# A graph layer on one core: 92 rows of main edges in 46 iterations, 54 early chunks in place of 71, and a new order at both ends of the loop

## The chip, the cores and the metric

The kernel runs on one core of a Trainium2 chip. The metric is the device time of one execution in microseconds (us), the median of several runs of the same program. The core has a matrix engine (TensorE, "PE" in the profile, with its weight loads as "PEld"), a vector engine (DVE), a scalar engine (ACT), GpSimd (POOL) and SyncE (SP). Each engine works through its own queue in the order of the program, and they meet only at semaphores.

## What is computed

A graph with N = 6250 nodes, 128 features and E = 106,250 edges, sorted by their destination `dst`; the last N edges of the unsorted list are loops from a node to itself. Every edge has one of three types.

```python
src_x = node_feature[edge_src]
parts = [relu(node_feature)]
for t in range(3):
    msg = relu(src_x @ W_e[t].T + b_e[t])
    msg = where(edge_type == t, msg, 0)
    parts.append(segment_sum(msg, edge_dst, num_segments=N))
agg = concatenate(parts, axis=1)
for t in range(3):
    updated = where(node_type == t, agg @ W_n[t].T + b_n[t], updated)
x = layernorm(x + updated + node_feature)
```

## The kernel before

**The table.** A message depends on the source node and the type alone, so PE, ACT and SP first build `message_table` in DRAM, N * 3 rows of 128 numbers (`make_batch`, `relu_half`, `store_half`, `store_last`). An edge is then a gather of one row.

**Main edges.** The first MAIN = HR * R = 90 * 1080 edges lie as 90 rows on 90 partitions. DVE removes the loops and 128 "dense" edges of each row (64 from each of two sets of 640 source nodes), closes the rows up to 896 slots (`close_up`, `unpack`, L1102 to L1105) and prepares indices and keys. PE turns them (`setup_unit`, L1556) and ACT copies them to `idx_t` and `key_t` (L798). The loop has NI = 45 iterations of two rows. An iteration has 14 columns, in four groups of 3, 4, 3 and 4: POOL gathers each column of 128 rows with one indirect DMA (L753), DVE makes the one-hots of a group (`one_hot`, L1252), PE sums the group with them (`sum_group`, L1652), and DVE adds the sums to `acc` (`add_sums`, L1264). The message buffer and the one-hots exist once, so POOL waits before it gathers group g of iteration j for the sum of group g of iteration j - 1:

```python
if j > 0:
    pool.wait_ge(group_summed, NG * (j - 1) + g + 1)
```

**Early edges.** The other 9,050 edges are ET = 71 chunks of 128. POOL gathers their rows of `x` into `xg` (L749) while the table is built, the calls from the 27th on held back by `msg_made`. PE turns, multiplies and sums them in NE = 36 pairs, one in each of the first iterations (`early_turn` L1614, `early_make` L1626 to L1631, `early_sum` L1640).

**Dense edges.** DVE picks two lists of 64 for each row (`list_dense`, L1131 and L1133, eight rounds each, run one after the other), unpacks them (`unpack_dense`, L1137 to L1146, whose L1142 signals `dense_keyed`), and later compares them with node numbers (`dense_onehot`, L1328). PE turns the keys (`dense_keys`, L1658), and for each iteration runs `dense_turn` (L1673), `dense_make` (L1686, L1690) and `dense_sum` (L1698). The turns come once in four quarters, and from iteration LEAD_FROM on once in three, so that the last is done in time.

**Tiles.** The 6250 nodes are 49 tiles of 128. Four are "extra": their edges are all early ones, and they use buffer set 1. A tile goes through ACT `finish_x` (L896), ACT `mask_selfs` (L912, the loops' messages), PE `finish_turn` (L1736) and `place_selfs` (L1713), DVE `finish_acc` (L1399), PE `finish_linear` (L1747, L1748 and the six of L1755), DVE `finish_h` (L1367 to L1375), ACT `finish_sd` (L917), DVE `finish_y` (L1381, L1383) and an SP store (L552, L568). `tile_step` puts tile t at iteration t + 3. Five tiles, 40 to 44, are still open in the last iteration, written out by hand as `last_iteration` on each engine.

**Order at the start of the loop.** On PE, `quarter(0, 0)` is `sum_group(0, 0)`, then `dense_keys()`, and only then `sum_group(0, 1)`. `dense_turn(0)` stands at the end of quarter (0, 3), ahead of `sum_group(1, 0)`. The change leaves these lines as they are:

```python
sum_group(j, g)
if q == 0:
    dense_keys()
```

Of the kernel before, what the change touches and what calls it, by code (L numbers as in the profile page):

```python
# [34 lines left out]
P = 128  # L35
# [5 lines left out]
R, HR, HC = 1080, 90, 7  # L41
# [3 lines left out]
KE = 4  # L45
# [54 lines left out]
SIDES = 2  # L100
# [17 lines left out]
QUADS = (NA - 1) // QUAD  # L118
BATCHES = ([(0, 1)] + [(1 + QUAD * m, QUAD) for m in range(QUADS)] + [(1 + QUAD * QUADS, NA - 1 - QUAD * QUADS)])
TAKEN_LATE, LATE = 3, 4  # L120
SPLIT = NA - TAKEN_LATE
Z0_TILES = SPLIT + 1
STORES = len(BATCHES) - 1 + TAKEN_LATE
SETS_OF_TILES = 4
assert sum(n for _, n in BATCHES) == NA and BATCHES[-1] == (SPLIT, TAKEN_LATE)
# [19 lines left out]
LEAD_FROM, LEAD_STEP = NE, 3  # L145
# [27 lines left out]

LIMIT_STEP = 15
# [12 lines left out]
LINEAR_AT = [next(q for q in range(at + 2, at + 6) if q % NG == 2) for at in EXTRA_AT]  # L187
# [6 lines left out]
assert PAIR_OF[-1] == NE - 1 and SLOT_OF[KE] + 1 + T <= ET  # L194


def tile_step(q, later):
    t = (q - later) // NG - (LATE - 1)
    return t if (q - later) % NG == 0 and 0 <= t < SPLIT else None
# [32 lines left out]
def build(nc, x, src, dst, etype, ntype, w_e, b_e, w_n, b_n, out):  # L232
# [6 lines left out]
    with ExitStack() as ctx:  # L239
# [59 lines left out]
        xg = sb("xg", [P, ET, D])  # L299
# [94 lines left out]
        iota_moved = sem("iota_moved")  # L394
        hot_iota_set, acc_zeroed, limits_set = sem("hot_iota_set"), sem("acc_zeroed"), sem("limits_set")
# [101 lines left out]
        def _(sp):  # L497
# [168 lines left out]
            for tile, tiles in BATCHES:  # L666
                if NI <= tile + tiles + LATE and tile + tiles <= SPLIT:
                    sp.wait_ge(fin_y[0], tile + tiles)
                    store_fin(tile, tiles)
            sp.wait_ge(fin_y[2], 1)  # L670
            store_fin(SPLIT)
            sp.wait_ge(fin_y[0], Z0_TILES)
            store_fin(SPLIT + 1)
            sp.wait_ge(ctl_set, 1)
            need = sp.value_load(ctl[0:1, 0:1], min_val=0, max_val=1)
# [37 lines left out]
        def _(pool):  # L713
# [13 lines left out]
                      allow_small_or_imprecise_dtypes=True)  # L727
# [54 lines left out]
        def _(act):  # L782
# [136 lines left out]
            def quarter(j, g):  # L919
# [13 lines left out]
                if g == 2 and j > 1:  # L933
                    mask_selfs(j - 2)
# [5 lines left out]
            def last_iteration():  # L940
                finish_x(0, 2, first=True)
                mask_selfs(SPLIT + 1)
                mask_selfs(SPLIT + 2)
                mask_selfs(ORDER[KE])
                finish_x(Z0_TILES - 1)
# [4 lines left out]
                finish_sd(Z0_TILES - 1)  # L950
# [22 lines left out]
        def _(dve):  # L973
# [151 lines left out]
            def list_dense(s):  # L1125

                for k in range(DENSE // 8):
# [754 lines left out]
```

## Time and profile before

| what | us |
|---|---|
| median of 3 runs (905.99 to 906.22) | 906.05 |
| the profiled execution | 907.5 |
| its span, first to last instruction | 905.7 |
| PE busy in it | 716.2 (79%) |
| POOL busy in it | 673.7 (74%) |
| DVE busy in it | 616.4 (68%) |
| mean granted TensorE clock | 0.912 |

Busy time leaves out the time in which an engine's sequencer prepares or waits. A row of the timeline has the start, the length, the engine, the line, the operation, what it writes and reads, its shape and how many instructions were merged; in brackets stand the engine's idle time before it and what ended it ("issue": nothing that the profile shows).

### The profile page before, as it was taken

How to read it: one execution, taken by the hardware profiler on the slowest of the kernel's cores; microseconds unless marked ns; L12 is line 12 of the kernel's file. 1: busy time of each engine (PE TensorE's matmuls, PEld its weight loads, DVE VectorE, ACT ScalarE, POOL GpSimd, SP SyncE). 2: the span in 40 equal slices, each digit the busy share in tenths (PEclk: the TensorE clock that was granted, in tenths of full speed). 3: DMA queues.
4: the chain of work that ended last, by engine and by line, in shares of the span. 5: the costliest groups of instructions: out<-in, count | busy, mean ns of one | idle time of the engine just before them, and what ended most of it. 6: DMA issues, size and time to landing. Idle time of an engine off the chain costs nothing.

```text
span 905.7 us, 14050 instructions
## 1 busy us (share of the span) xinstructions
PE 716.2 (79%) x4555; PEld 598.9 (66%) x4555; DVE 616.4 (68%) x1468; ACT 145.0 (16%) x397; POOL 673.7 (74%) x719
## 2 busy tenths in 40 slices
PE   5593056887997988888898878989888798769786
PEld 3362056776876876676687766878767587658674
DVE  7999988476676557557575754775675477656656
ACT  3393000111111101111110120110112011001120
POOL 7777777777777777777777777777777777777772
PEclk9796569998999989999999998999899999989989
DMA  8595533433443343343344342434435334324321
GB/s 245 161 311 147 136 97 76 113 97 50 146 117 105 97 110 107 103 111 92 94 118 116 96 115 78 121 107 111 106 96 114 93 85 118 102 63 128 97 53 45
DMA packets 72065, 101.39 MB, mean 112 GB/s; under 512 B 18137, under 2 KB 55517, under 8 KB 71995
## 3 DMA queue, kind: packets, MB, share of 16 engines
q0 software_dynamic: 22432, 45.99, 21.3%
q1 hardware_dynamic: 46861, 50.45, 18.5%
q10 hardware_dynamic: 2702, 4.08, 1.5%
q8 instruction: 37, 0.61, 0.3%
q14 instruction: 33, 0.27, 0.1%
HBM read 87.47 MB, written 12.97 MB: 111 GB/s over the span
## 4 chain that ended last, share of the span: by engine, by line
POOL 44%; PE 18%; issue 16%; DVE 15%; DMA 6%; SPq 0%; DVEq 0%; POOLq 0%; ACT 0%; ACTq 0%
POOL tab L753 44%; DMA tab<-message_table,idx_t 5%; PE ps L1652 5%; PE ps L1755 3%; PE ps L1673 3%; DVE src_wide L1098 1%; DVE stage L1131 1%; PE ps L1690 1%; PE ps L1686 1%; DVE first_wide L1034 1%; PE ps L1748 1%; DMA dst_raw<-in_dst 1%; PE ps L1631 1%; DVE dst_raw L1091 1%; PE ps L1698 1%
## 5 line engine op out<-in xcount | busy, mean ns | idle before, releaser
L753 POOL DMA_INDIRECT tab<-message_table,idx_t x630 | 595.2, 945 | 194.1 <-issue 185.6
L1652 PE MATMUL ps<-work,tab 128*128 128x126 f32 x1260 | 180.4, 286 | 94.0 <-DMA tab<-message_table,idx_t 68.7
L1252 DVE TENSOR_TENSOR work<-key_t,ps 128x378 f32<-128x378 f32 (+1 forms) x180 | 108.8, 606 | 208.3 <-PE ps L1652 203.7
L1652 PEld LDWEIGHTS ps<-work,tab 128*128 128x128 f32 x1260 | 163.6, 199 | 106.2 <-issue 68.4
L1264 DVE TENSOR_TENSOR acc<-ps,acc 128x126 f32 (+1 forms) x306 | 96.2, 314 | 30.0 <-DVE acc L1264 9.9
L1755 PE MATMUL ps<-wn_t,stage 128*128 128x384 f32 x282 | 104.8, 512 | 0.0
L749 POOL DMA_INDIRECT xg<-in_x,esrc_t x67 | 72.4, 1081 | 20.7 <-issue 16.8
L1755 PEld LDWEIGHTS ps<-wn_t,stage 128*128 128x128 f32 x282 | 56.3, 200 | 40.4 <-issue 5.6
L1673 PE MATMUL ps<-first_wide,tab 128*128 128x128 f32 x450 | 62.8, 291 | 9.5 <-DVE first_wide L1328 6.5
L1673 PEld LDWEIGHTS ps<-first_wide,tab 128*128 128x128 f32 x450 | 58.9, 207 | 9.9 <-issue 9.9
L896 ACT ACTIVATE stage<-ps 128x128 f32<-128x128 f32 x47 | 12.9, 277 | 297.0 <-PE ps L1755 282.1
L1673 PE MATMUL ps<-dense_f,tab 128*128 128x128 f32 x450 | 60.0, 283 | 0.0
L1673 PEld LDWEIGHTS ps<-dense_f,tab 128*128 128x128 f32 x450 | 56.6, 200 | 0.0
L1370 DVE SCALAR_TENSOR_TENSOR h<-ps,mask,h 128x128 f32<-128x128 f32 x147 | 51.6, 351 | 6.7 <-PE ps L1755 1.5
L1626 PE MATMUL ps<-we_t,emsg 128*128 128x128 f32 x216 | 36.3, 312 | 23.0 <-issue 20.4
L917 ACT ACTIVATE sd<-mv,eps 128x1 f32<-128x1 f32 x49 | 14.3, 294 | 230.2 <-DVE mv L1375 230.2
L1626 PEld LDWEIGHTS ps<-we_t,emsg 128*128 128x128 f32 x216 | 32.0, 220 | 27.0 <-issue 23.8
L1686 PE MATMUL ps<-we_t,order_f 128*128 128x128 f32 x270 | 44.1, 308 | 6.5 <-DVE acc L1264 6.5
L1573 PE MATMUL ps<-we_t,work 128*128 128x384 f32 x98 | 44.5, 540 | 3.3 <-DVEq L995 3.2
L1686 PEld LDWEIGHTS ps<-we_t,order_f 128*128 128x128 f32 x270 | 40.7, 225 | 8.1 <-issue 7.8
L1690 PE MATMUL ps<-we_t,order_f 128*128 128x128 f32 x270 | 44.2, 302 | 0.0
L1338 DVE TENSOR_TENSOR order_f<-ps,dst_raw 128x768 f32<-128x768 f32 x45 | 42.7, 949 | 0.1
(260 smaller groups left out, 1021.4 us busy)
## 6 DMA issues: line engine op xcount, KB each, us to landing
tab<-message_table,idx_t POOLq DMA_INDIRECT x630, 2.6
message_table<-tab SPq DMA_DIRECT2D x24, 384.0 KB, 3.5
dst_raw<-dense_types SPq DMA_DIRECT2D x45, 192.0 KB
wn_raw<-message_table SPq DMA_DIRECT2D x22, 384.0 KB, 3.4
src_wide<-dense_lists SPq DMA_DIRECT2D x45, 128.0 KB, 3.2
we_raw<-early_types SPq DMA_DIRECT2D x18, 192.0 KB
be_b<-early_types SPq DMA_DIRECT2D x18, 192.0 KB
work<-in_x ACTq DMA_DIRECT2D x10, 256.0 KB, 5.0
```

Of the source, the lines that this page charges most:

```text
L749: pool.indirect_dma_start(xg[:, q, :], None, x, bass.IndirectOffsetOnAxis(ap=rows, axis=0)).then_inc(x_gathered, 16)
L753: pool.indirect_dma_start(msg[:, slot, :], None, table, bass.IndirectOffsetOnAxis(ap=rows, axis=0)).then_inc(signal, 16)
L1252: dve.tensor_tensor(hot[:, first:first + n, :].rearrange("p c (t w) -> p c t w", w=WIN), keys.broadcast_to((P, n, T, WIN)), iota_win.rearr ...
L1264: dve.tensor_tensor(cols, sums.rearrange("p (t c) -> p t c", t=T), cols, ALU.add).then_inc(added, 1)
L1370: fin_link(dve.scalar_tensor_tensor(h[z][:, :], lin_bank(z, nth)[:, t * D:(t + 1) * D], mask[:, t, at(tile)], h[z][:, :], ALU.mult, ALU.ad ...
L1573: pe.matmul(ps[:, MSG_PS + i, 0:T * D], xt[:, par, i, :], we_t[:, :], start=True, stop=False)
L1626: pe.matmul(early_made[:, 0, :], exm[:, 0, t, :], we_t[:, t * D:(t + 1) * D], start=(t == 0), stop=False)
L1652: ins = pe.matmul(sums_bank(j, g), msg[:, column, :], hot[:, column, :], start=(c == 0), stop=(c == n - 1))
L1673: ins = pe.matmul(dxt_ps[:, :, s * DENSE:(s + 1) * DENSE], dx[:, (SETS - 1 - s) * DT + k, :], donehot[s][:, k, :, :], start=(k == 0), stop ...
L1686: pe.matmul(dmsg_ps[:, 0, :], dxm[:, 0, t, :], we_t[:, t * D:(t + 1) * D], start=(t == 0), stop=False)
L1690: ins = pe.matmul(dmsg_ps[:, 1, :], dxm[:, 1, t, :], we_t[:, t * D:(t + 1) * D], start=False, stop=(t == T - 1))
L1755: ins = pe.matmul(lin, stage[z][:, i, :], wn_t[:, i, :], start=False, stop=(i == T))
```

## The change

HR goes from 90 to 92 and KE, the number of extra tiles, from 4 to 3. From this follow NI = 46, MAIN = 99,360, ET = 54, NE = 27, and 644 table gathers and 54 early gathers where there were 630 and 71. PE waits for `masks_set` after the turning of indices and keys, no more before it. DVE does four rounds of the first dense list, then the one-hots of iteration 0, then the other twelve rounds. Tiles are laid out by `tile_turns`: as before up to tile 33, and from tile 34 on up to one iteration sooner. LEAD_FROM is NI - 9 = 37 (36 before). In the last iteration four tiles are open, 42 to 45, none but tile 45 waits for the last group's sum, and the order of all engines is new.

```diff
-R, HR, HC = 1080, 90, 7
+R, HR, HC = 1080, 92, 7
-KE = 4
+KE = 3
-QUADS = (NA - 1) // QUAD
+QUADS = (NA - 3) // QUAD
-TAKEN_LATE, LATE = 3, 4
+TAKEN_LATE, LATE = 2, 4
-LEAD_FROM, LEAD_STEP = NE, 3
+LEAD_FROM, LEAD_STEP = NI - NG * 2 - 1, 3
+def tile_turns():
+    at = []
+    for t in range(SPLIT):
+        if t < LEAD_FROM - LATE + 1:
+            at.append(NG * (t + LATE - 1))
+        else:
+            at.append(max(NG * (t + LATE - 2), turn_at(t + 1) + ADD_LATER - ACC_LATER, at[-1] + NG - 1))
+    return at
+def tile_step(q, later):
+    return TILES.get(q - later)
@@ sync, the last stores
-            sp.wait_ge(fin_y[2], 1)
-            store_fin(SPLIT)
-            sp.wait_ge(fin_y[0], Z0_TILES)
-            store_fin(SPLIT + 1)
+            sp.wait_ge(fin_y[0], Z0_TILES)
+            store_fin(SPLIT - 1)
             sp.wait_ge(ctl_set, 1)
             need = sp.value_load(ctl[0:1, 0:1], min_val=0, max_val=1)
-            store_extra(KE)
+            sp.wait_ge(fin_y[2], 1)
+            store_fin(SPLIT)
             sp.wait_ge(fin_y[3], 1)
             store_fin(NA - 1)
+            store_extra(KE)
@@ vector, finish_h
+                if isinstance(nth, int) and nth > 0:
+                    dve.wait_ge(fin_y[z], nth)
@@ vector, last_iteration
                 dve.wait_ge(group_summed, NG * j + 2)
-                finish_h(SPLIT - 1, SPLIT - 1)
-                dve.wait_ge(group_summed, NG * j + 3)
                 add_sums(j, 0, bases_of[0])
                 add_sums(j, 1, bases_of[1])
-                finish_acc(SPLIT + 1, Z0_TILES - 1, 0, ADDED["main", j, 1])
+                finish_acc(NA - 1, 0, 3, ADDED["main", j, 1])
+                finish_h(SPLIT - 1, SPLIT - 1)
                 finish_h(SPLIT, 0, 2)
+                finish_y(SPLIT - 1, SPLIT - 1)
+                dve.wait_ge(group_summed, NG * j + 3)
                 add_sums(j, 2, bases_of[2])
-                finish_y(SPLIT - 1, SPLIT - 1)
                 finish_y(SPLIT, 0, 2)
+                finish_h(NA - 1, 0, 3)
                 dve.wait_ge(group_summed, NG * j + 4)
                 add_sums(j, 3, bases_of[3])
                 finish_acc(ORDER[KE], KE, 1, ALL_ADDS)
-                finish_acc(NA - 1, 0, 3, ALL_ADDS)
-                finish_h(SPLIT + 1, Z0_TILES - 1)
+                finish_y(NA - 1, 0, 3)
                 finish_h(ORDER[KE], KE, 1, slot=SLOT_OF[KE])
-                finish_y(SPLIT + 1, Z0_TILES - 1)
-                finish_h(NA - 1, 0, 3)
                 finish_y(ORDER[KE], KE, 1, slot=SLOT_OF[KE])
-                finish_y(NA - 1, 0, 3)
@@ vector, ahead of the loop
-            list_dense(0)
-            list_dense(1)
+            list_dense(0, range(DENSE // 16))
             dve.wait_ge(iota_moved, 1)
             dve.wait_ge(setup_copied, len(UNITS))
             for g in range(NG):
                 one_hot(0, g)
+            list_dense(0, range(DENSE // 16, DENSE // 8))
+            list_dense(1, range(DENSE // 8))
             unpack_dense()
@@ tensor, last_iteration, from the second group on
                 sum_group(j, 1)
-                finish_linear(0, 2, first=True)
-                pe.wait_ge(stage_acc[2], 1)
-                finish_turn(SPLIT + 1, Z0_TILES - 1, len(BATCHES))
                 pe.wait_ge(added, ADDED["dense", j, SIDES - 1])
                 finish_turn(NA - 1, 0, len(BATCHES), 3, first=True)
                 pe.wait_ge(fin_var[1], KE)
                 finish_turn(ORDER[KE], KE, NZ, 1)
+                place_selfs(NA - 1, 0, 3)
+                place_selfs(ORDER[KE], KE, 1)
+                finish_linear(0, 2, first=True)
                 pe.wait_ge(added, ADDED["main", j - 1, NG - 1])
                 sum_group(j, 2)
-                place_selfs(SPLIT + 1, Z0_TILES - 1)
-                place_selfs(NA - 1, 0, 3)
-                place_selfs(ORDER[KE], KE, 1)
+                finish_linear(0, 3, first=True)
                 pe.wait_ge(hot_ready, NG * NI)
                 pe.wait_ge(d_hot, NI)
+                linear_open(KE, 1)
                 pe.wait_ge(added, ADDED["main", j, 1])
-                linear_open(KE, 1)
                 sum_group(j, 3)
-                finish_linear(Z0_TILES - 1)
                 linear_types(KE, 1)
-                finish_linear(0, 3, first=True)
@@ tensor, ahead of the loop
-            pe.wait_ge(masks_set, 1)
             pe.wait_ge(tab_ready, 2 * NB + 1)
             pe.wait_ge(rows_set, 1)
             setup_unit(IDX_UNIT, KEY_UNIT)
             pe.wait_ge(keys_set, 1)
             setup_unit(KEY_UNIT, len(UNITS))
+            pe.wait_ge(masks_set, 1)
```

Besides this, `xg` is kept large enough for the extra tiles' slots, the batches of tile loads are cut as (2, then 4 each, then 3), and POOL makes the limit that row 91 is held against with one more small instruction. In the main loop `finish_linear` stands ahead of `place_selfs`.

## Rows read from the trace of the kernel before

**Rows 1.** The page: busy time of each engine, and the group of the table gathers.
```profile
PE 716.2 (79%) x4555; PEld 598.9 (66%) x4555; DVE 616.4 (68%) x1468; ACT 145.0 (16%) x397; POOL 673.7 (74%) x719
...
L753 POOL DMA_INDIRECT tab<-message_table,idx_t x630 | 595.2, 945 | 194.1 <-issue 185.6
```

**Rows 2.** Timeline of POOL: the 54th early gather, the first table gather.
```profile
78.46 1.18 POOL L749 DMA_INDIRECT xg<-in_x,esrc_t  x1 [0.30 <-issue]
...
101.54 0.94 POOL L753 DMA_INDIRECT tab<-message_table,idx_t  x1 [0.30 <-issue]
```

**Rows 3.** Waits of POOL: total us, times, longest.
```profile
POOL tab L753 <- PE ps L1652: 8.4, 21, 1.1
```

**Rows 4.** Timeline of POOL: table gathers 18, 29, 564 and the last, 630.
```profile
122.79 0.94 POOL L753 DMA_INDIRECT tab<-message_table,idx_t  x1 [0.30 <-issue]
...
136.53 0.94 POOL L753 DMA_INDIRECT tab<-message_table,idx_t  x1 [0.30 <-PE ps L1652]
...
805.58 0.94 POOL L753 DMA_INDIRECT tab<-message_table,idx_t  x1 [0.85 <-PE ps L1652]
...
889.53 0.94 POOL L753 DMA_INDIRECT tab<-message_table,idx_t  x1 [0.30 <-issue]
```

**Rows 5.** Timeline of PE, from the turned indices to the second iteration.
```profile
88.50 1.28 PE L1556 MATMUL ps<-ident,first_wide 90*128 90x90 f32 x7 [14.38 <-DVE mask L1245]
...
114.74 1.65 PE L1652 MATMUL ps<-work,tab 128*128 128x126 f32 x6 [23.19 <-DVE work L1252]
...
117.55 0.41 PE L1658 MATMUL ps<-ident,stage 90*128 90x90 f32 x1 [1.16 <-DVE stage L1142]
...
117.75 4.20 PE L1652 MATMUL ps<-work,tab 128*128 128x126 f32 x22
...
128.70 2.48 PE L1673 MATMUL ps<-first_wide,tab 128*128 128x128 f32 x10 [6.52 <-DVE first_wide L1328]
...
133.10 3.14 PE L1652 MATMUL ps<-work,tab 128*128 128x126 f32 x20
```

**Rows 6.** Timeline of ACT: indices copied to `idx_t`.
```profile
89.22 1.42 ACT L798 ACTIVATE idx_t<-ps 128x270 int32<-128x270 f32 x2 [13.43 <-PE ps L1556]
```

**Rows 7.** Timeline of DVE over the same stretch.
```profile
82.97 0.62 DVE L1104 TENSOR_SCALAR first_wide<-loop_f 90x896 f32<-90x896 int32 x1
...
117.20 0.29 DVE L1142 SCALAR_TENSOR_TENSOR stage<-stage 90x128 f32<-90x128 int32 x1
...
120.37 0.55 DVE L1252 TENSOR_TENSOR work<-key_t,ps 128x378 f32<-128x378 f32 x1 [1.10 <-PE ps L1652]
...
128.47 0.82 DVE L1328 TENSOR_TENSOR dense_f<-src_wide,ps 128x640 f32<-128x640 f32 x1
```

**Rows 8.** Sums of one stretch: engines' busy us, granted clock, DMA share, GB/s.
```profile
100.00:120.00 20.00, 4.10 (x18) 3.81 (x19) 18.32 (x45) 1.81 (x1) 15.13 (x16) 0.50 0.28 73
```

**Rows 9.** Timeline of PE: the last extra tile's linear in the leading stretch.
```profile
795.84 0.32 PE L1747 MATMUL ps<-bn_parts,pick_parts 128*128 128x384 bf16 x1 [3.17 <-DVE mv L1375]
...
796.65 3.79 PE L1755 MATMUL ps<-wn_t,stage 128*128 128x384 f32 x6
```

**Rows 10.** Timeline of the end: PE, DVE, the last store.
```profile
884.33 0.33 PE L1747 MATMUL ps<-bn_parts,pick_parts 128*128 128x384 bf16 x1
...
885.13 2.10 PE L1755 MATMUL ps<-wn_t,emsg 128*128 128x384 f32 x6
...
892.19 0.49 PE L1652 MATMUL ps<-work,tab 128*128 128x126 f32 x2 [0.31 <-DMA tab<-message_table,idx_t]
...
893.14 0.56 DVE L1399 TENSOR_TENSOR stage<-acc,ps 128x384 f32<-128x384 f32 x1
...
900.21 1.12 DVE L1370 SCALAR_TENSOR_TENSOR h<-ps,mask,h 128x128 f32<-128x128 f32 x3 [0.36 <-PE ps L1755]
...
902.69 0.35 DVE L1383 TENSOR_SCALAR xg<-h,mv,rstd 128x128 f32<-128x128 f32 x1
...
903.52 0.36 SPq L552 DMA_DIRECT2D out<-xg  x1
```

More of the change, by code:

```diff
@@ L186 @@
 EXTRA_AT = [extra_at(n) for n in range(KE)]
-LINEAR_AT = [next(q for q in range(at + 2, at + 6) if q % NG == 2) for at in EXTRA_AT]
+LINEAR_AT = [next(q for q in range(at + 2, at + 8)
+                  if (q % NG == 2 or q >= NG * LEAD_FROM) and tile_step(q, LINEAR_LATER) is None
+                  and tile_step(q - 1, LINEAR_LATER) is None) for at in EXTRA_AT]
 EXTRAS = {at: n for n, at in enumerate(EXTRA_AT)}
@@ L193 @@
 assert all(LIMIT_FIRST + LIMIT_STEP * (PAIR_OF[n] + 1) >= (NA + 2 + n) * P for n in range(KE - 1))
[L194 to L199, printed above, removed]
+assert PAIR_OF[-1] == NE - 1 and SLOT_OF[KE] + 1 + T <= NT + 2 * (1 + T)
 def count_adds():
@@ L932, in quarter @@
                     dense_relu(dense_step(q, MAKE_LATER))
-                if g == 2 and j > 1:
-                    mask_selfs(j - 2)
+                if tile_step(q, -2) is not None:
+                    mask_selfs(tile_step(q, -2))
+                if q == NG * (NI - 1) - 2:
+                    mask_selfs(SPLIT)
                 if q + 2 in EXTRAS:
@@ L1123, in spans, with list_dense @@
                 dve.tensor_tensor(tail, tail, penalty[:, :], ALU.add).then_inc(keys_set, 1)
-            def list_dense(s):
-                for k in range(DENSE // 8):
+            def list_dense(s, rounds):
+                for k in rounds:
                     first, last = dense_window(k)
@@ L1437, in quarter @@
                     self_masks()
-                if tile_step(q, ACC_LATER) is not None:
-                    finish_acc(tile_step(q, ACC_LATER), tile_step(q, ACC_LATER), 0, ADDED["main", j - 1, NG - 1])
+                t = tile_step(q, ACC_LATER)
+                if t is not None:
+                    finish_acc(t, t, 0, max(ADDED["main", t + 1, NG - 1], ADDED["dense", t + 1, SIDES - 1]))
                 if q - 1 in EXTRAS:
@@ L1764, in batches_up_to @@
             def batches_up_to(tile):
-                return sum(first <= max(tile, 1) for first, _ in BATCHES)
+                return sum(first <= max(tile, BATCHES[1][0]) for first, _ in BATCHES)
             def quarter(j, g):
@@ L1785, in quarter @@
                     finish_linear(t, first=t == 0, behind=extras if extras else None)
+                t = tile_step(q, 1)
+                if t is not None:
+                    place_selfs(t, t)
                 if q in EXTRA_LINEAR:
                     n = EXTRA_LINEAR[q]
-                    done = sum(tile_step(before, LINEAR_LATER) is not None for before in range(q))
+                    done = sum(tile_step(before, LINEAR_LATER) is not None for before in range(q + 1))
                     finish_linear(n, 1, first=n == 0, behind=done)
```

31 lines of the change are left out of this document (16 added, 15 removed).

## The prediction

> **What bounds the kernel now.** I read the page first, and there PE looks like the busiest engine, 79% against POOL's 74% [rows 1]. That is misleading: each table gather counts 0.945 us as busy, and in front of nearly every one stand 0.30 us more that wait for nothing, 185.6 of the 194.1 us of idle time in that group [rows 1]. So I read POOL's timeline next. A gather costs 1.25 us from start to start, the first table gather starts at 101.54 [rows 2] and the last at 889.53 [rows 4]. These are 629 steps in 787.99 us, 1.253 each: POOL practically never stops from the beginning of the kernel to 16 us before its end. The view of waits says how much it waits for others: 21 times for PE's sums, 8.4 us in total [rows 3]. Each such entry holds the usual 0.30, so the real part is 8.4 - 6.3 = 2.1 us; the one at gather 564 shows 0.85 where 0.30 is usual [rows 4]. Take the 2.1 out of the stretch from gather 29 to gather 630 (136.53 to 889.53, 601 steps [rows 4]) and a free step is 750.9 / 601 = 1.2494 us. PE and DVE can be late only by making POOL wait, and after POOL's last gather.
>
> So the change is judged by three numbers: when POOL gets going, how many gathers it then has to issue, and what is left behind the last.
>
> **The counts.** 71 early gathers become 54 and 630 table gathers 644: three fewer in all, 3.7 us. This gain exists only if POOL starts its table gathers 17 steps sooner and is not stopped afterwards.
>
> **When the first table gather can start.** POOL ends the 54th early gather at 79.6 [rows 2]; I leave the pace up to there as it is. The table isn't what it waits for: its last part is sent before that, and in the trace of before nothing was waited for at 101.54. The indices are. DVE writes them until 82.97 + 0.62 = 83.6 [rows 7], but PE turns them only at 88.50, 14.38 us idle, released by the masks [rows 5]. With the wait for the masks moved behind, PE starts at 83.8, ACT's two copies end (89.22 + 1.42) - 88.50 = 2.14 later [rows 5, 6], at 85.9, and POOL starts at about 86.2, 15.3 us sooner. The same two turns and copies run as before, only 4.7 us sooner. What else is pulled ahead of the masks, the keys, must still wait for DVE's key work and is hidden under the lists.
>
> **What stops it: the 18th gather.** POOL then has free columns for iteration 0 (14) and, once group 0 of iteration 0 is summed, for 3 more. The new place of the one-hots buys just that: they are there half a list after 88, around 98, well ahead of gather 15 at 86.2 + 14 * 1.25 = 103.7. Gather 18 would start at 107.4. It belongs to group 1 and waits for the sum of group 1 of iteration 0. On PE `dense_keys` stands in front of that sum, and it waits for `dense_keyed`, which DVE signals after all sixteen rounds of both lists. In the trace this is seen directly: PE does the six records of group 0 at 114.74, then is released by DVE's L1142 for the transpose at 117.55, and only at 117.75 goes on [rows 5]; L1142 starts at 117.20 [rows 7]. Neither the lists' rounds nor the four one-hots get fewer or shorter: windows of the lists go by R = 1080, and DVE works 18.32 of the 20 us from 100 to 120 [rows 8]. So `dense_keyed` stays at 117.5. The sum of group 1 is 8 of the 22 records of 4.20 us from 117.75 on, 1.5 us, or 2.2 at the pace of 114.74 (six in 1.65) [rows 5]. With the usual 0.30, gather 18 starts at 119.6 to 120.3; I take 120.0. Before, it started at 122.79 [rows 4]. POOL stands for some 12.6 us, and of 15.3 us only 2.8 are left. This also answers what the moved waits cost: up to 12 us of delay of the indices would not be seen.
>
> **The 29th gather.** It is the first of iteration 2 and waits for the sum (1, 0). That sum is on PE behind `dense_turn(0)`, which starts at 128.70 after 6.52 us of idleness, released by DVE's one-hot of L1328 [rows 5, 7], and the sum starts at 133.10 [rows 5]. DVE is the pacer here: its chain of key work, lists, row bases (the 1.10 us before 120.37 [rows 7]; the sum named there had ended at 116.4) and loop lists doesn't change. The sum's six records take 0.94 us as their share of 20 in 3.14, or 1.65 as at 114.74 [rows 5]: done at 134.0 to 134.75, gather 29 at 134.3 to 135.1, taken as 134.8. By POOL's own pace it would be 120.0 + 11 * 1.25 = 133.7, so the wait decides. Before it was 136.53 [rows 4]. What is left of the earlier start is 1.7 us, and it can be between 1.4 and 2.2.
>
> PE runs this stretch at the lower of its two clock levels: granted 0.50 in 100:120 [rows 8], 1.2 GHz. The Trainium skill ("TensorE: Matmul & The Clock Gate", section "Part 1: The HAM clock gate") has the throttled clock as the default, which activity releases; by that rule the sum pulled ahead to 98 doesn't help, since PE is idle again until 117.5. The trace agrees, with 0.50 after 23.19 us of idleness; at full clock `dense_turn(0)` would be over some 2 us sooner and so would gather 29, and the sum would be 2 us less.
>
> **The loop.** From gather 29 there are now 644 - 29 = 615 steps: 615 * 1.2494 = 768.4, so the last gather starts at 134.8 + 768.4 = 903.2. The early work ends 9 iterations sooner, but it was PE's and DVE's and hidden under POOL: nothing.
>
> **The 2.1 us of stalls** came around gather 564, where the fourth extra tile's linear stood in the stretch of three-quarter turns: PE waited 3.17 us for DVE at 795.84 and its next six matmuls took 3.79 us at the fallen clock, 2.10 elsewhere [rows 9, 10]. That tile is gone, and so is this cause (it is already out of the 1.2494). New in its place is one more main tile in the nine last iterations. A tile's linear is 2.9 us of PE (884.33 to 887.23 [rows 10]), spread over some 150 us; I see no single place where it piles up. New stalls lie between 0 and the 2.1 of before; I take 0.5. Last gather: 903.7. The new `fin_y` wait in `finish_h` is for DVE's own earlier instruction, two quarters back: nothing.
>
> **The end.** Before, the kernel ended 905.7 - 889.53 = 16.2 us after the last gather started [rows 4, 10]: landing and sum at +2.7 (892.19), then on PE two whole linears and a half one. Now tile 44 needs no sum of the last two groups, and behind the last sum stands only half a linear. But PE has the other linears ahead of it. From the end of group 1's sum, at -5.2 (884.33), it does eight transposes (1.4 by estimate, 1.0 to 2.0), a linear (2.75), group 2 (0.8, half of the 1.65 at half clock), a linear (2.75), the opening of tile 45 (885.13 - 884.33 = 0.8), group 3 (1.0): it is through at +4.3 instead of +3.15. From there: DVE's last add and `finish_acc` (892.68 to 893.70: 1.0), six matmuls (1.95), DVE and ACT from L1370 to the tile's end (900.21 to 903.04: 2.85, and 0.1 before), the store (905.7 - 903.52 = 2.2) [rows 10]. Sum: 12.4. If PE weren't the bound, 11.3; if it waits on ACT or DVE as well, up to 14.5.
>
> **Sum.** 903.7 + 12.4 = 916.1 for the span of 905.7: +10.4. Against the profiled execution's own 907.5 that is 917.9; the 1.8 around the span stays. That execution lay 1.45 above the median of the runs, so the median becomes 906.05 + 10.4 = 916.4. In short: fourteen gathers more, +17.5; start, -1.7; old stalls, -2.1, new ones, +0.5; end, -3.8.
>
> **Rivals.**
> 1. *POOL runs through (faster).* If nothing stopped it from 86.2 on, the last gather would start at 86.2 + 643 * 1.2494 = 889.6, the end come at 902.0, the median at 902.3. The point from which this decides is `dense_keyed` at 107.4 or sooner, together with the dense turn ten us sooner. For it speaks that indices, table and group 0 are ready; against it 117.20 and 117.55 in [rows 5, 7], and that I find no instruction taken out of that chain.
> 2. *The leading stretch stalls more.* With early work gone after iteration 26, PE has less to do in ten iterations, its clock may fall in more of them, and then the closer tiles meet a slow PE, as at 796.65, where six matmuls lost 1.7 us and the waits came to 2.1 [rows 3, 9]. Two or three such events cost 2 to 5 us: 918.5 to 921. The same page of the Trainium skill speaks for it: idleness brings the clock down. Against it: POOL's lead over PE is refilled in each iteration, and three extra tiles earlier in the loop cost nothing.
> 3. *The end isn't shortened*, because PE's pile of linears in front of the last sum takes as long as what was taken from behind it: +3.8, 920.2.
> 4. *Nothing measurable*: needs a chain on DVE ten us shorter without POOL being free throughout, for which nothing speaks.
>
> **Chances.** The forecast 0.76, with a range of its own from 914.5 to 918.5 (start 1.4 to 2.2, new stalls 0 to 2.1, end 11.3 to 14.5). Rival 1: 0.05. Rival 2: 0.10. Rival 3: 0.07. Rival 4: 0.02. A change of 0.2% (1.8 us) is about what a measurement of this kernel can tell from none. Slower is the forecast with rivals 2 and 3: 0.93; faster 0.05; same 0.02. The range is 913.5 to 920.5: it takes in the forecast, rival 3 and the lower half of rival 2.
>
> **What would show it.** In the new trace: POOL's first table gather near 86.2 with an idle time of some 6 us before it, released by ACT's copy; an idle time of about 12 us before the 18th, released by PE, with PE's transpose near 117.5 just ahead; a wait of 1 us before the 29th, at 134.8; the last gather near 903.5; the end some 12.4 us after. The prediction is wrong if gather 18 starts long before 119, if the loop's step isn't 1.25, or if POOL's waits after gather 29 come to more than 2 us.

## The result and the profile after

The changed kernel takes 940.77 us (median of 4 runs, 935.38 to 942.1), the one before, measured beside it, 906.13 (905.99 to 906.55): 1.037 times as long, 95% interval 1.0328 to 1.0412. Forecast were 916.4 and a range up to 920.5. The change is slower, as forecast, but by 34.6 us and not by 10.4. The ratios leave out slow runs, of which there was one below, 3772.36 us for the kernel with its loads cut into 75 and 15 rows.

The page of the profiled execution (its own time 941.7; line numbers of the changed kernel, the table gather is L773 now):

```profile
span 939.8 us, 13789 instructions
...
PE 724.6 (77%) x4451; PEld 606.0 (64%) x4451; DVE 609.4 (65%) x1455; ACT 142.7 (15%) x389; POOL 667.4 (71%) x717
...
L773 POOL DMA_INDIRECT tab<-message_table,idx_t x644 | 608.3, 945 | 233.8 <-issue 191.4
```

Against [rows 1], POOL's share fell from 74% to 71%. POOL, which paced the kernel before, has stood still somewhere. Its timeline shows where:

```profile
84.81 0.94 POOL L769 DMA_INDIRECT xg<-in_x,esrc_t  x1 [0.30 <-PE ps L1594]
...
101.51 1.07 POOL L773 DMA_INDIRECT tab<-message_table,idx_t  x1 [15.75 <-ACT idx_t L818]
...
135.09 0.94 POOL L773 DMA_INDIRECT tab<-message_table,idx_t  x1 [12.55 <-PE ps L1672]
...
149.49 0.94 POOL L773 DMA_INDIRECT tab<-message_table,idx_t  x1 [0.97 <-PE ps L1672]
...
810.51 0.94 POOL L773 DMA_INDIRECT tab<-message_table,idx_t  x1 [1.64 <-PE ps L1672]
...
826.55 0.94 POOL L773 DMA_INDIRECT tab<-message_table,idx_t  x1 [2.61 <-PE ps L1672]
...
831.95 0.94 POOL L773 DMA_INDIRECT tab<-message_table,idx_t  x1 [1.96 <-PE ps L1672]
...
844.18 0.94 POOL L773 DMA_INDIRECT tab<-message_table,idx_t  x1 [3.80 <-PE ps L1672]
...
926.91 0.94 POOL L773 DMA_INDIRECT tab<-message_table,idx_t  x1 [0.30 <-issue]
```

The shape at the start is the forecast one: a wait for ACT's copy of the indices before the first table gather, 12.55 us before the 18th, 0.97 before the 29th, each released by what was named. But each of them is late: 101.51 for the forecast 86.2, 135.09 for 120.0, 149.49 for 134.8. After the 29th come five waits for PE between 810 and 850: 1.64, 2.61, 1.96, 3.80 and, at 849.47, 0.60, each with the usual 0.30 in it, 9.1 us net.

The span grew by 34.1 us. Of this the 29th gather gives +13.0 (149.49 against 136.53 in [rows 4]), fourteen more steps of 1.2494 give +17.5, stalls after the 29th gather +6.9 (926.91 - 149.49 - 615 * 1.2494 = 9.0, where before had 2.1), the tail -3.3 (939.8 - 926.91 = 12.9 for 16.2). Against the forecast span of 916.1, 23.7 us are unaccounted for: 14.7 at the 29th gather, 8.5 in stalls, 0.5 in the tail.

**Why the start is late.** DVE's first instruction on the edges waits for four transfers that SP issues: the three loads of destinations, sources and types, and behind them one number for each row (0.4 KB), the destination that follows the row's last:

```profile
4.32 0.33 SPq L531 DMA_DIRECT2D dst_raw<-in_dst  x1
...
5.44 0.56 SPq L532 DMA_DIRECT2D dst_raw<-in_dst  x1
```

The chain of waits names the fourth, which goes by the same tile name (start, length, what), and DVE waits for it:

```profile
5.44 23.72 DMA dst_raw<-in_dst
```

```profile
29.18 1.27 DVE L1046 TENSOR_REDUCE low<-dst_raw 92x1 f32<-92x1080 int32 x1 [17.80 <-DMA dst_raw<-in_dst]
```

Before, the same piece of the chain, and the sizes of its transfers with the time from issue to landing, read:

```profile
5.62 7.38 DMA dst_raw<-in_dst
...
13.02 1.27 DVE low L1027
```

```profile
dst_raw<-in_dst SPq DMA_DIRECT2D x1, 379.7 KB, 4.7
...
typ_raw<-in_edge_type SPq DMA_DIRECT2D x1, 379.7 KB, 7.2
...
dst_raw<-in_dst SPq DMA_DIRECT2D x1, 0.4 KB, 7.4
```

DVE starts 16.2 us later. The 29th gather comes 120.3 us after DVE's start, and the forecast had put it at 134.8 - 13.0 = 121.8. It was the three loads that became slow. In the trace's own records of DMA packets each row of 1080 numbers is one packet of 4320 bytes. Before, the 270 rows of the three loads move from 6.77 to 11.87 us; in the changed kernel the 276 rows move from 6.59 to 28.02. The loads are 2% larger and take four times as long.

**Why POOL stalls late.** PE's waits from 740 to 880 (sum in us, times, longest):

```profile
PE ps L1756 <- DVE stage L1420: 15.8, 4, 5.6
```

L1756 is `finish_turn`, and L1420 the last instruction of DVE's `finish_acc` for the tile before. `finish_turn` writes the PSUM columns that this `finish_acc` still has to read, so PE waits for it. PE's own timeline, and DVE's over the same stretch:

```profile
811.13 1.72 PE L1672 MATMUL ps<-work,tab 128*128 128x126 f32 x14
...
818.45 0.45 PE L1756 MATMUL ps<-ident,xg 128*128 128x128 f32 x1 [5.59 <-DVE stage L1420]
...
836.17 0.45 PE L1756 MATMUL ps<-ident,xg 128*128 128x128 f32 x1 [3.82 <-DVE stage L1420]
```

```profile
810.27 0.68 DVE L1271 TENSOR_TENSOR work<-key_t,ps 128x504 f32<-128x504 f32 x1 [6.36 <-PE ps L1672]
...
816.11 0.55 DVE L1271 TENSOR_TENSOR work<-key_t,ps 128x378 f32<-128x378 f32 x1 [0.85 <-issue]
...
817.75 0.56 DVE L1420 TENSOR_TENSOR stage<-acc,ps 128x384 f32<-128x384 f32 x1 [0.28 <-DVE acc L1283]
```

PE ends two groups' sums at 812.85, then stands until DVE has worked through one quarter (from 810.27) and most of the next (from 816.11), where `finish_acc` of the tile before ends at 817.75 + 0.56. DVE began only at 810.27, having stood 6.36 us for a sum of PE's. So the two take turns in waiting, and the next sum, and with it POOL's next free columns, is behind `finish_turn` in PE's queue.

`finish_acc` of a tile stands two quarters behind its `finish_turn`. With tiles four quarters apart PE therefore has two quarters between that `finish_acc` and the next tile's turn, with three apart only one. The changed kernel has four such short steps, at tiles 34, 35, 37 and 38, and the wait occurs four times.

### The profile page after: what moved, and what is told of

It is laid out like the page before. It is cut to its first block, busy times and chain, and to the rows that moved or that the text cites. A ratio compares the mean times of both kernels' runs of the same rounds, so it can differ in the third digit from the quotient of the medians.

```text
span 939.8 us, 13789 instructions
## 1 busy us (share of the span) xinstructions
PE 724.6 (77%) x4451; PEld 606.0 (64%) x4451; DVE 609.4 (65%) x1455; ACT 142.7 (15%) x389; POOL 667.4 (71%) x717
## 4 chain that ended last, share of the span: by engine, by line
POOL 42%; PE 19%; DVE 17%; issue 16%; DMA 5%; DVEq 1%; SPq 0%; ACT 0%; ACTq 0%
POOL tab L773 42%; PE ps L1693 4%; PE ps L1672 4%; PE ps L1775 3%; DMA dst_raw<-in_dst 3%; DMA tab<-message_table,idx_t 2%; PE ps L1710 2%; PE ps L1706 1%; DVE src_wide L1117 1%; DVE stage L1150 1%; PE ps L1768 1%; DVE h L1391 1%; DVE acc L1283 1%; DVE first_wide L1053 1%; PE ps L1718 1%
## 5 line engine op out<-in xcount | busy, mean ns | idle before, releaser
L773 POOL DMA_INDIRECT tab<-message_table,idx_t x644 | 608.3, 945 | 233.8 <-issue 191.4
L1672 PE MATMUL ps<-work,tab 128*128 128x126 f32 x1288 | 190.2, 293 | 86.7 <-DMA tab<-message_table,idx_t 75.1
L1672 PEld LDWEIGHTS ps<-work,tab 128*128 128x128 f32 x1288 | 173.1, 204 | 101.4 <-issue 90.7
L1693 PE MATMUL ps<-first_wide,tab 128*128 128x128 f32 x460 | 69.2, 306 | 6.0 <-DVE first_wide L1347 5.5
L769 POOL DMA_INDIRECT xg<-in_x,esrc_t x50 | 53.2, 1064 | 24.5 <-PE ps L1594 13.2
L1693 PEld LDWEIGHTS ps<-first_wide,tab 128*128 128x128 f32 x460 | 65.5, 222 | 6.5 <-issue 6.5
L1693 PEld LDWEIGHTS ps<-dense_f,tab 128*128 128x128 f32 x460 | 59.4, 205 | 0.0
L1706 PE MATMUL ps<-we_t,order_f 128*128 128x128 f32 x276 | 47.1, 317 | 6.8 <-DVE acc L1283 6.8
L1710 PE MATMUL ps<-we_t,order_f 128*128 128x128 f32 x276 | 47.5, 313 | 0.0
L932 ACT ACTIVATE wn_raw<-wn_raw,smask 128x128 f32<-128x128 f32 x135 | 43.8, 390 | 0.0
L1718 PE MATMUL ps<-first_wide,dense_f 128*128 128x216 f32 x184 | 41.4, 347 | 1.6 <-DVE first_wide L1367 1.6
```

What stands on the lines that cost most here:

```text
L769: pool.indirect_dma_start(xg[:, q, :], None, x, bass.IndirectOffsetOnAxis(ap=rows, axis=0)).then_inc(x_gathered, 16)
L773: pool.indirect_dma_start(msg[:, slot, :], None, table, bass.IndirectOffsetOnAxis(ap=rows, axis=0)).then_inc(signal, 16)
L1672: ins = pe.matmul(sums_bank(j, g), msg[:, column, :], hot[:, column, :], start=(c == 0), stop=(c == n - 1))
L1693: ins = pe.matmul(dxt_ps[:, :, s * DENSE:(s + 1) * DENSE], dx[:, (SETS - 1 - s) * DT + k, :], donehot[s][:, k, :, :], start=(k == 0), stop ...
L1706: pe.matmul(dmsg_ps[:, 0, :], dxm[:, 0, t, :], we_t[:, t * D:(t + 1) * D], start=(t == 0), stop=False)
L1710: ins = pe.matmul(dmsg_ps[:, 1, :], dxm[:, 1, t, :], we_t[:, t * D:(t + 1) * D], start=False, stop=(t == T - 1))
```

## The experiments

Two theories were put against the slowdown. A: the loads of the edges are slow because of their number of rows, 92. B: the late stalls come from `finish_turn` standing right behind the sum in the stretch where tiles are three quarters of an iteration apart. Rival to A: any load of this size with more rows, or the other work pulled forward, does it. Rival to B: the lower clock, or DVE's amount of work.

The Trainium skill ("DMA: Bandwidth & Descriptors", section "Why a DMA increments its semaphore by 16 and not by 1") says that a transfer is spread over the largest number of engines, at most 16, that divides the slowest dimension of both its sides: 15 for 90 rows, 4 for 92, 16 and 12 for 80 and 12. That named theory A. No view names the engines of one transfer, but the packet records show how many rows of edges are in flight at once. In the changed kernel it is four at most for 21.3 of the 21.4 us; in the kernel before 15 is the commonest number (2.2 of 5.1 us). The trace agrees with the rule.

**The load in two parts**, in the changed kernel, rows 0 to 79 and 80 to 91. DVE now waits for seven transfers, not four; the last of them, the 92 single numbers, is left as it was:

```diff
-sp.dma_start(raw[:, :], dram[0:MAIN].rearrange("(p c) -> p c", c=R)).then_inc(got_edges, 16)
+for first, last in ((0, 80), (80, HR)):
+    sp.dma_start(raw[first:last, :], dram[first * R:last * R].rearrange("(p c) -> p c", c=R)).then_inc(got_edges, 16)
```

> The changed kernel with one edit: each of the three loads of edges is sent as two, rows 0 to 79 and rows 80 to 91, where it was one of 92 rows. Theory A (the number of rows of one load decides over how many DMA engines it is spread; 90 rows divide by 15, 92 by 4 at most, 80 by 16, 12 by 12): the loads land near 13 us again where they land at 29.2, DVE begins its chain near 13, POOL's 18th table gather starts near 120 (135.1 now) and the 29th near 135 (149.5 now), and the median falls by 15 us to about 926. Rival (the loads are late for another reason, such as the ACT queue's own loads at that time or the 2% more bytes): DVE still begins at 27 or later and the median stays near 940.

Measured: 927.9 (923.42 to 929.73), 1.0216 of before (1.0188 to 1.0243), 12.9 us under the changed kernel.

```profile
16.97 1.27 DVE L1048 TENSOR_REDUCE low<-dst_raw 92x1 f32<-92x1080 int32 x1 [4.89 <-DMA dst_raw<-in_dst]
...
PE ps L1758 <- DVE stage L1422: 17.6, 4, 5.6
```

DVE starts 12.2 us sooner, the 29th gather comes at 137.58, 11.9 sooner. The rows of the loads now end at 12.68, and 15 or 16 of them are in flight for 2.6 of 6.4 us. The late waits (here L1758 and L1422) are untouched. Theory A held, with 12.9 us where 15 was expected: the start lies 4 us later than the expected 13; 9.2 us of stalls stay.

**The same in the kernel before**, loads cut into 76 and 14 rows (by the rule 4 and 14 engines):

> The kernel before with one edit: its three loads of edges are sent as rows 0 to 75 and rows 76 to 89, where each was one load of 90 rows. 76 rows divide by 4 at most, 14 by 14. Theory A: most of the bytes go as slowly as in the changed kernel; DVE begins its chain 10 to 16 us later than at 13.0, everything up to POOL's 29th table gather moves by as much, and the median rises by 10 to 16 us, to 916 to 922. Rival (size or count of loads does not matter): 906, within 1 us.

Measured: 918.07, 1.0123 (1.0106 to 1.014), 11.2 us over before (906.85 in that batch), with 90 rows and nothing else changed. The rows of the loads end at 27.94, for 11.87 in the kernel before.

```profile
29.35 1.27 DVE L1029 TENSOR_REDUCE low<-dst_raw 90x1 f32<-90x1080 int32 x1 [17.23 <-DMA dst_raw<-in_dst]
```

**Cut into 75 and 15 rows** instead, as many transfers:

> The kernel before with its three loads of edges sent as rows 0 to 74 and rows 75 to 89. It has as many loads as the run that sent 76 and 14 rows, and both 75 and 15 divide by 15. Theory A: DVE starts on the edges at 13 to 17 us and the median is 905 to 908. Rival (the number of loads, not the divisor, cost the 11 us): 915 or more.

```profile
14.13 1.27 DVE L1029 TENSOR_REDUCE low<-dst_raw 90x1 f32<-90x1080 int32 x1 [2.02 <-DMA dst_raw<-in_dst]
```

Measured: 908.12 against 908.38, ratio 0.9993 (0.9983 to 1.0003). Neither the cutting nor a part of some 75 rows costs anything measurable; how the number of rows divides does.

**The kernel before once more**, for its spread:

> The kernel before, unchanged, profiled once more beside the three others of this group. DVE's first instruction on the edges starts at 13.0 us in the profile of before and at 16 to 17 in four of the five variants with whole or split fast loads. If that is the chip and the moment, this profile will have it at 15 to 17 as well, with a span within 1 us of 906; if it is something of the changed kernel, it will have it at 13.0 to 13.5.

Measured: 909.18 in one run, DVE's first instruction at 14.59 (13.02 in the profile shown). Over all kernels with 90 undivided rows this start lies between 13.0 and 16.1, with 92 rows cut 80 and 12 between 15.9 and 17.0. Most of that spread is the fourth transfer. With 90 rows in the changed kernel (the next run, DVE at 16.05) the types land as soon as before, 7.5 us after issue for 7.2, and the single numbers 3 us later:

```profile
typ_raw<-in_edge_type SPq DMA_DIRECT2D x1, 379.7 KB, 7.5
...
dst_raw<-in_dst SPq DMA_DIRECT2D x1, 0.4 KB, 10.4
```

With 92 rows cut 80 and 12 the rows of the loads end between 12.2 and 14.3 us and DVE starts 2.5 to 4.3 us behind them; with 90 rows uncut it is 1.2 to 2.0. Cutting the fourth transfer too was not tried.

**90 rows in the changed kernel** (HR 90, KE 4, all else as changed):

> The changed kernel with HR and KE set back to 90 and 4, and so 630 table gathers, 71 early ones and 45 iterations; the start's and the end's new order and the sooner tiles stay. Theory: the first table gather starts at 101.5 as before and the 29th at 136.5; the tail after the last gather is about 12.5 instead of 16.2; the sooner tiles bring POOL waits in the stretch of three-quarter turns, 5 to 10 us in place of 2.1. Sum: 906 - 3.7 + 3 to 8 = 905 to 910. Rival (POOL's waits there come from PE's thinner work after iteration 27 and not from the tiles' places): they stay near 2 us and the median is 902 to 903.

Measured: 927.32, 1.0222 (1.0205 to 1.0239). The expectation of 905 to 910 was missed. The start is mended (DVE at 16.05, 29th gather 137.03), but POOL stalls 26 us after it:

```profile
PE ps L1756 <- DVE stage L1420: 16.1, 4, 4.5
...
PE ps L1767 <- DVE mv L1396: 5.8, 1, 5.8
```

The short steps are four here too, and PE's waits at them as long as with 92 rows (16.1 us for 15.8), so the closer turns are costly without the 92 rows. New is the wait of 5.8 us: a fourth extra tile stands in this stretch, and its linear is one quarter ahead of a main tile's. POOL's longest stall, 7.6 us, lies right behind that wait.

**The turn at the end of PE's quarter** (with the load in two parts):

```diff
-                if t is not None:
+                if t is not None and q < NG * LEAD_FROM:
                     finish_turn(t, t, batches_up_to(t), first=t == 0)
...
+                t = tile_step(q, 0)
+                if t is not None and q >= NG * LEAD_FROM:
+                    finish_turn(t, t, batches_up_to(t))
```

> The kernel of the split load with one edit: in the stretch of three-quarter turns PE does a tile's finish_turn as the last thing of its quarter, behind linear, dense make and dense turn, where it stood right behind the group's sum. Theory B (POOL's waits in that stretch come from PE standing at finish_turn for DVE's finish_acc of the tile before, which with tiles three quarters apart belongs to the quarter just ended): PE's waits for DVE's finish_acc there, 17.6 us with the split load, fall under 5, POOL's waits after its 29th gather fall from 9.2 us to under 4, the median falls by 5 us or more. Rival (they come from the fallen clock and the thin work on PE whatever the order): POOL's waits stay at 7 to 11 us, the median within 2 us of the split load's.

Measured: 919.84 (919.21 to 921.85), 1.015 (1.0129 to 1.017), 8.1 us under the kernel with the loads cut alone.

```profile
PE ps L1758 <- DVE stage L1422: 1.5, 1, 1.5
```

17.6 us of waits became 1.5, and POOL's stalls after the 29th gather became nothing, with no matmul and no instruction of DVE's removed. Theory B held. The clock moved with it. The window from 800 to 860 in the kernel with only the loads cut, and in this one (window, length, busy time of PE, its loads, DVE, ACT and POOL, granted clock, DMA share, GB/s):

```profile
800.00:860.00 60.00, 48.02 (x293) 40.98 (x292) 36.49 (x87) 5.87 (x21) 39.38 (x43) 0.89 0.34 87
```

```profile
800.00:860.00 60.00, 53.02 (x339) 45.34 (x338) 38.79 (x91) 7.01 (x25) 45.36 (x49) 0.92 0.40 104
```

The clock rose from 0.89 to 0.92 once PE stood less, and in the kernel before it is 0.93 there. So the lower clock goes with the waits; what share of the 8.1 us came through it wasn't measured by itself.

The size of the stalls isn't fixed. Four kernels have the same order in this stretch, and their profiled executions have 9.1 us of stalls (the changed kernel), 9.2 (loads cut), 3.6 and 5.3 (the two edits at the start, below). The runs of each of them spread over 3.8 to 6.7 us, with the turn moved over 2.6. That the one makes the other is likely, but only one execution of each kernel has a profile.

**The tiles elsewhere**: the load in two parts, and the tiles brought forward one quarter each at tiles 28, 32, 38 and 41, four quarters apart otherwise. This line takes the place of the `if` and `else` in `tile_turns`:

```diff
+at.append(NG * (t + LATE - 1) - sum(t >= sooner for sooner in (28, 32, 38, 41)))
```

> The kernel of the split load with other tile turns: each of the tiles 28, 32, 38 and 41 comes a quarter sooner after its forerunner and all others four quarters apart, where the changed kernel has five steps of three quarters from tile 34 to 38. The last tiles have the places they have in the changed kernel. Theory B: most steps are four quarters again; POOL's waits after its 29th gather fall from 9.2 us to 1 to 5, the median falls by 4 to 8 us. Rival (fallen clock, thin work): they stay at 7 to 11 us.

Measured: 923.38, 1.0181 (1.0164 to 1.0198). The stalls fell from 9.2 to 1.4 (1.45 and 0.50, less the usual 0.30 each), but the tail grew from 12.8 to 15.0: 4.5 us better than the close turns, 3.5 worse than moving the instruction. The expectation counts five short steps in the changed kernel; by its `tile_turns` they are four, as many as here, but close together there. PE's waits for `finish_acc` from 540 to 900, and the window from 800 to 860:

```profile
PE ps L1755 <- DVE stage L1419: 15.8, 6, 4.6
...
800.00:860.00 60.00, 50.63 (x315) 43.08 (x314) 33.21 (x79) 7.19 (x24) 45.37 (x49) 0.89 0.39 100
```

PE still waits 15.8 us for `finish_acc`, six times, and POOL hardly notices. So such a wait alone isn't the price; it is paid where the waits follow each other closely. And the granted clock is 0.89, as low as with the loads alone cut, while POOL works 45.37 us of the 60 for 39.38: the lower clock by itself doesn't stop POOL there.

**The same with 90 rows** (27, 31, 37, 40, uncut loads). The edit also loosens the rule for the extra tiles' linears, which puts the third extra tile's at quarter 137, one ahead of a main tile's (138 in the other kernels with 90 rows):

```diff
-                  if (q % NG == 2 or q >= NG * LEAD_FROM) and tile_step(q, LINEAR_LATER) is None
+                  if (q % NG == 2 or q >= NG * 27) and tile_step(q, LINEAR_LATER) is None
```

> The changed kernel with 90 rows and 4 extra tiles, and the tile turns spread as in the run beside it (a quarter sooner at tiles 27, 31, 37 and 40). Nothing is left of the change but the start's order, spread sooner tiles and the new last iteration. Theory B: POOL's waits, 26 us in the run with 90 rows, fall to 1 to 6 us, the tail after the last gather is 12.5 to 13.5 us where it was 16.2 before; the median is 903 to 908. Rival (the extra tile at iteration 38 is what makes the 26 us): they stay above 12 us, the median above 914.

Measured: 937.18, 1.0334 (1.0317 to 1.0352); missed by far, and the rival's numbers came true. POOL stalls 34 us. PE's waits from 540 to 900:

```profile
PE ps L1764 <- DVE mv L1393: 17.5, 5, 5.4
...
PE ps L1753 <- DVE stage L1417: 15.2, 6, 3.3
```

L1764 begins a tile's linear and waits until DVE has the statistics of the tile whose sums share its PSUM bank. With four extra tiles among the moved ones this handover is too close as well. How much of the 34 us is the tile count and how much the third linear's new place wasn't separated, and PE also stood 13.0 us, four times, for nothing that the profile shows.

**90 rows, with the turn and the extra tile's linear last:**

> The changed kernel with 90 rows and 4 extra tiles, and in the stretch of three-quarter turns PE does finish_turn and the extra tile's linear as the last things of their quarter. Theory B: POOL's waits, 26 us with 90 rows alone, fall under 4 us, the tail after the last gather is 12.5 to 14; the median is 902 to 908, 20 us under the run with 90 rows alone. Against the kernel with 92 rows and finish_turn last (919.8) the fourteen gathers and the later start of the table gathers weigh 13 to 18 us. Rival: with a fourth extra tile there the waits stay above 10 us whatever the order, 915 or more.

Measured: 918.65, 1.011 (1.0095 to 1.0125), where 902 to 908 was expected. The turn's waits are gone (L1756 1.1 in all), the next one in line is not:

```profile
818.43 0.48 PE L1767 MATMUL ps<-bn_parts,pick_parts 128*128 128x384 bf16 x1 [5.78 <-DVE mv L1396]
```

One quarter behind the extra tile's linear comes a main tile's, and waits 5.78 us for DVE's statistics of the former. POOL stalls 16.3 us in all, 8.9 of them right behind this wait; the 7.4 ahead of it weren't traced to a cause. The rival had it right here: above 10 us and 915 or more, whatever the order.

**The start undone** (the loads cut, `masks_set` and the one-hots where they were before):

> The kernel of the split load with the two edits at the start undone: PE waits for the masks ahead of the turning of indices, and the one-hots of iteration 0 stand behind both lists. Theory of the prediction (the 18th and the 29th gather are held by the dense keys and the dense turn, whatever lies ahead of them): gathers 18 and 29 start within 0.5 us of where they do with the split load alone, and the medians agree within 1 us. Rival (the edits save what they were put in for): the 29th gather and the median are 2 us or more later than with the split load alone.

Measured: 929.35 (924.5 to 930.95), 1.0254 (1.0237 to 1.0271). The 29th gather comes 120.4 us after DVE's start, 120.6 with the edits, so they save nothing there; only the stop moves, to the 15th gather, which waits 8.55 us (with the usual 0.30). The medians lie 1.45 us apart (1 was expected), less than either kernel's own spread.

**`dense_keys` later on PE** (the loads cut, at quarter 2 instead of 0):

> The kernel of the split load with one edit: PE turns the dense keys two quarters later, after the sum of group 2 of iteration 0. Theory of the prediction (the dense keys hold the 18th gather, the dense turn and DVE's next one-hots hold the 29th): the 18th gather starts by 12 us or more sooner than the 123.3 of the split load, as soon as POOL reaches it, and the 29th no sooner than 0.5 us; the median is within 1.5 us of the split load's. Rival (the stop at the 18th gather is what costs): the 29th gather starts 2 us or more sooner too, and the median falls with it.

Measured: 926.32, 1.0225 (1.0203 to 1.0247).

```profile
109.94 0.94 POOL L775 DMA_INDIRECT tab<-message_table,idx_t  x1 [0.30 <-issue]
...
122.18 0.94 POOL L775 DMA_INDIRECT tab<-message_table,idx_t  x1 [3.80 <-PE ps L1674]
...
136.34 0.94 POOL L775 DMA_INDIRECT tab<-message_table,idx_t  x1 [9.47 <-PE ps L1674]
```

The 18th gather starts 13 us sooner and waits for nothing. The wait turns up 7 and 11 gathers later instead (3.50 and 9.17 us net), and the 29th is 120.5 us behind DVE's start as ever. The median is 1.6 us under that of the loads cut alone, where 1.5 was the limit expected; the runs of the two kernels overlap, and DVE started 1.1 us sooner in this profile. So removing a stop before the one that DVE sets gained nothing measurable.

**Where the old 2.1 us were.** The prediction laid them on the extra tile's linear. In the kernel before, that linear alone last in its quarter:

> The kernel before with one edit: the linear of the extra tile in the stretch of three-quarter turns stands last in its quarter on PE. Theory: PE's wait of 3.2 us for DVE there goes, POOL's three waits near its 564th to 578th gather, 2.0 us together, go with it, and the median falls by 1 to 2 us, to 904 to 905.5. Rival (the waits come from the fallen clock of that stretch, not from the place of the linear): the median stays within 0.5 us of before.

```profile
PE ps L1747 <- DVE mv L1375: 3.2, 1, 3.2
```

Measured: 908.06 against 908.38, 0.9999 (0.9988 to 1.0009); the 3.2 us wait hasn't changed, so the theory fell. The wait belongs to the main tile's linear that follows in the same bank. With all linears of the stretch last:

> The kernel before with all linears of the stretch of three-quarter turns, the main tiles' and the extra tile's, as the last things of their quarter on PE. In the run where only the extra tile's linear was moved, the wait of 3.2 us for DVE stayed; by the order of the quarters it belongs to the main tile's linear of two quarters later, which shares a PSUM bank with the extra one and waits for DVE to have read it. Theory: with dense make and dense turn ahead of it, that wait falls under 1 us, POOL's three waits of 2.0 us together go, and the median falls by 1 to 2 us. Rival (the 2 us come from another wait of that stretch, such as the 5.0 us for DVE's add ahead of a dense make): the wait at the linear goes and POOL's waits and the median stay within 0.5 us.

Measured: 905.99 against 906.66, 0.9992 (0.9983 to 1.0002). The wait is gone and POOL's last gather starts at 887.26 (889.53 in [rows 4]), but behind it the kernel needs 18.0 us for 16.2. 2 us of POOL's time were there to be had, and PE's heap of work at the end takes them back: PE is through its last matmul at 899.9 us, where it was at 900.1.

No kernel was measurably faster than before.

## Why the prediction missed, step by step

**The step that failed: "DVE's chain ... doesn't change"** and, for POOL, "I leave the pace up to there as it is". Both took for granted that DVE starts at 13.0. In the list of counts HR went from 90 to 92 and I priced only the gathers and the windows, not the three loads whose row count it is. 29.18 for 13.02: this one unpriced term is 14.7 of the 23.7 us, and by the experiment 12.9 of the time. It is the larger cause. It reached further than DVE's chain: the 54th early gather, forecast to start where it did before, at 78.46, started at 84.81, and at 78.34 with the loads cut.

**The term that was mis-sized: new stalls, "between 0 and the 2.1 of before; I take 0.5".** They were 9.0. "I see no single place where it piles up" looked at the amount of PE's work, 2.9 us a tile. What matters is the order: at three quarters apart `finish_turn` comes one quarter after DVE's `finish_acc` of the tile before instead of two, and stands directly behind the sum, ahead of all of PE's other work of the quarter. PE waits for DVE, POOL for PE. Rival 2 had the place and the sign right, with 2 to 5 us, but it began with a fallen clock for want of work; the runs show it begins with an instruction's place in the queue. Moving that one instruction removed the stalls at the same amount of work, and the clock came back with them; spreading the tiles removed nearly all of them at the low clock of 0.89.

**The cause given for the old 2.1 us** was wrong in detail: not the extra tile's linear, but the wait of the next main tile's for that tile's statistics.

**The forecast's own range was drawn too narrow.** Its three terms at their worst (start 1.4, stalls 2.1, end 14.5) add up to 920.4, and not to the 918.5 given. The measured time lies far outside both.

**Held:** the direction, by the cause given for it, fourteen gathers more. The first table gather waits for ACT's copy. The 18th waits for `dense_keys`: PE's transpose stands just ahead, after 18.98 us of idleness, released by DVE:

```profile
112.04 1.62 PE L1672 MATMUL ps<-work,tab 128*128 128x126 f32 x6 [7.86 <-DVE work L1271]
...
132.64 0.42 PE L1678 MATMUL ps<-ident,stage 92*128 92x92 f32 x1 [18.98 <-DVE stage L1161]
...
132.85 4.96 PE L1672 MATMUL ps<-work,tab 128*128 128x126 f32 x22
```

(forecast wait 12.6, measured 12.55 with the usual 0.30 in it). The 29th is DVE's: 120.3 to 121.1 us behind DVE's start in all kernels with 92 rows, for 121.8. How early the indices are did not matter. A step costs 1.2494 us: with it the experiment without stalls adds up to its last gather, 137.65 + 615 * 1.2494 = 906.0 (906.05 measured). The fourteen gathers cost 17.5. The tail is 12.9 for 12.4, its last tile as worked out:

```profile
932.74 2.20 PE L1775 MATMUL ps<-wn_t,stage 128*128 128x384 f32 x6 [1.09 <-DVE stage L1420]
...
935.05 1.12 DVE L1391 SCALAR_TENSOR_TENSOR h<-ps,mask,h 128x128 f32<-128x128 f32 x3 [1.71 <-PE ps L1775]
...
937.72 0.33 SPq L585 DMA_DIRECT2D out<-xg  x1
```

**With both causes taken away** (loads cut, turn last) 919.8 us stand against the forecast 916.4. What is left is mainly the 29th gather at 137.65 for 134.8, since DVE starts at 16.7, not 13.0. So the other terms of the sum hold, but only for a kernel in which the loads stay fast and `finish_turn` stands elsewhere.

Not tried: giving the turned tile PSUM columns of its own, so that its place in the queue would not matter.

## What to carry to other kernels

When a row or partition count changes, list every transfer that has it as its outer dimension and see how it divides, before counting what the loops save; two rows more made the loads here take four times as long, at a place where nothing hid it. When a pipeline's distance is shortened, go through the queues instruction by instruction for those that now follow closely on what they wait for: the price is the round trip of two engines, not the instruction's length, and moving it to the end of the step may be enough. And if a wait sits ahead of another that the same engine's chain sets, removing it gains nothing, as here at the 18th gather.

## What the runs showed of the hardware

Loading the edges, three transfers of 388 KB in rows of 4.3 KB and one of 0.4 KB, lets DVE start at 29.2 us as 92 rows, at 15.9 to 17.0 as 80 and 12, and three of 380 KB at 13.0 to 16.1 as 90 rows, 14.1 as 75 and 15, 29.4 as 76 and 14. Rows in flight at once, by the packet records: at most four for nearly the whole load with 92 rows, most often 13 to 16 with 90 rows and with the fast cuts. While the slow loads run, the DMA engines aren't full: from 14 to 29 us their busy share is 0.65. Before, when these loads had landed and others ran, it was 0.84 (columns: window, length, busy time of the engines, granted clock, DMA share, GB/s).

```profile
14.00:29.00 15.00, 6.32 (x21) 3.98 (x20) 0.00 (x0) 3.01 (x5) 11.35 (x13) 0.78 0.65 209
```

```profile
14.00:29.00 15.00, 14.11 (x59) 8.69 (x57) 14.65 (x15) 8.00 (x13) 11.64 (x12) 1.00 0.84 271
```

The same program's start moved by 1.6 us between two profiled executions (13.02 and 14.59), about as much as the whole gain that the prediction gave to the start; the types' load landed 7.2 and 7.5 us after its issue in the two, the single numbers 7.4 and 9.0. A table gather's step of 1.25 us, 0.94 busy and 0.30 between, was the same in all kernels (a mean of 944 to 947 ns busy), whatever DVE and PE did beside it.
